# Placing half of batch 6 on TensorE, three copies moved to VectorE, and throw-away matmuls before the first placing

## The reference

```
xh = x.reshape(B, T, 16, 8); xc = xh - mean over tokens
corr = softmax(xc @ xc^T per head); x = layernorm(x + corr @ xh)

scores = sigmoid(x @ gate^T)                 # 64 experts, 8 groups of 8
4 groups are kept (by their two best), 8 experts in them are chosen
w = scores of the 8, normalized, * 2.5
each expert takes its first 128 tokens (CAP): xe[e, pos] = x[token]
ye = (silu(xe @ w1^T) * (xe @ w3^T)) @ w2^T  # F = 64
out = sum over a token's experts of w * ye   # + shared expert (F = 128)
x = layernorm(x + out)
```

## Time and profile before

| | us |
|---|---|
| median of 3 runs | 552.3 (550.35 to 553.13) |
| the profiled execution | 553.05 |
| its span | 550.8 |
| busy: PE, DVE, ACT, POOL | 415.4, 378.3, 365.9, 351.1 |

### The profile page before, as it was taken

One profiled execution on the slowest core, in us unless ns is written; L12 is line 12 of the kernel. 1 busy time (PEld: TensorE's weight loads), 2 busy tenths in 40 slices (PEclk: granted clock), 3 DMA queues, 4 the chain that ended last, 5 costly groups with the idle time before them and its releaser, 6 DMA issues.

```text
span 550.8 us, 9934 instructions
## 1 busy us (share of the span) xinstructions
PE 415.4 (75%) x3461; PEld 185.7 (34%) x3476; DVE 378.3 (69%) x1390; ACT 365.9 (66%) x486; POOL 351.1 (64%) x374
## 2 busy tenths in 40 slices
PE   3799998999898898898899889645699988740000
PEld 2323333333333333333333322123566666530000
DVE  7632769769769768768868638579877887730095
ACT  2699998998998898898998999610223322210056
POOL 3500000677777777777777777777768778888454
PEclk9699999999999999999999999965999999975555
DMA  3499990111000000000100100102366656334796
GB/s 95 139 220 222 349 388 20 52 40 46 24 6 21 14 3 19 12 3 2 27 3 2 26 3 1 24 2 63 78 121 101 112 92 96 36 36 38 150 291 194
DMA packets 71771, 43.69 MB, mean 79 GB/s; under 512 B 11859, under 2 KB 70964, under 8 KB 71329
## 3 DMA queue, kind: packets, MB, share of 16 engines
q1 hardware_dynamic: 51744, 36.18, 24.0%
q0 software_dynamic: 19968, 6.75, 10.5%
HBM read 21.27 MB, written 41.24 MB: 113 GB/s over the span
## 4 chain that ended last, share of the span: by engine, by line
DVE 29%; PE 23%; POOL 16%; ACT 14%; issue 9%; DMA 7%; ACTq 0%; DVEq 0%; POOLq 0%; SPq 0%
POOL records L571 10%; ACT large L1005 9%; PE PV L743 7%; PE S L727 5%; POOL sums L588 5%; DVE large L1587 4%; DMA sums<-centred,target 4%; PE M L645 3%; DVE LR L1261 2%; DVE centred L1644 2%; DMA records<-rec,index 2%; ACT OT L992 1%; PE M L674 1%; DVE last_stats L1672 1%; PE M L668 1%
## 5 line engine op out<-in xcount | busy, mean ns | idle before, releaser
L571 POOL DMA_INDIRECT records<-rec,index x224 | 225.4, 1006 | 141.0 <-DVE index L1404 70.4
L1005 ACT ACTIVATE large<-S,shift 128x1024 f32<-128x1024 f32 x256 | 273.4, 1123 | 23.3 <-PE S L727 21.1
L743 PE MATMUL PV<-large,V 128*9 128x512 f32 x1024 | 135.2, 600 | 0.0
L588 POOL DMA_INDIRECT sums<-centred,target x64 | 99.3, 1552 | 24.9 <-issue 12.2
L727 PE MATMUL S<-LR 64*128 64x512 bf16 x512 | 100.7, 392 | 13.4 <-ACT large L1005 9.0
L727 PEld LDWEIGHTS S<-LR 64*128 64x128 bf16 x512 | 24.6, 93 | 155.1 <-ACT large L1005 98.5
L863 PE MATMUL S<-large 128*128 128x512 bf16 (+1 forms) x189 | 42.6, 375 | 10.0 <-DVE large L1587 6.7
L1261 DVE COPY LR<-M 128x1024 bf16<-128x1024 bf16 x49 | 33.4, 681 | 16.9 <-PE M L645 16.9
L1587 DVE TENSOR_SCALAR large<-slot_c,large 128x128 bf16<-128x128 bf16 x256 | 43.7, 283 | 0.0
L1057 ACT COPY AK<-S 128x512 f32<-128x512 f32 (+1 forms) x17 | 9.5, 560 | 33.6 <-PE S L871 33.6
L863 PEld LDWEIGHTS S<-large 128*128 128x128 bf16 x204 | 19.1, 100 | 29.6 <-issue 9.8
(11 more groups left out here) (207 smaller groups left out, 672.1 us busy)
## 6 DMA issues: line engine op xcount, KB each, us to landing
records<-blank SPq DMA_DIRECT2D x1, 6176.0 KB, 32.2
large<-sums SPq DMA_DIRECT2D x24, 256.0 KB, 5.4
X<-records SPq DMA_DIRECT2D x15, 386.0 KB, 4.4
sums<-blank SPq DMA_DIRECT2D x2, 2112.0 KB
large<-L_ffn_w_dram SPq DMA_DIRECT2D x2, 2048.0 KB, 11.0
records<-rec,index POOLq DMA_INDIRECT x224, 2.1
X<-L_attn_x_dram SPq DMA_DIRECT2D x8, 256.0 KB, 2.9
w2s<-L_ffn_w_dram SPq DMA_DIRECT2D x1, 2048.0 KB, 17.5
```

Source lines behind the costliest of these rows:

```text
L571: pool.indirect_dma_start(records, bass.IndirectOffsetOnAxis(ap=index[:, i * TOP + k:i * TOP + k + 1], axis=0), rec[:, i, :], None, bounds ...
L588: pool.indirect_dma_start(sums[n % SUMS], bass.IndirectOffsetOnAxis(ap=target[:, u, i:i + 1], axis=0), ye[:, u, i, :], None, bounds_check= ...
L743: mm = pe.matmul(PV[g % 2][32 * i:32 * i + VCOLS, :], V[:, b % 2, 2 * c + k, QUAD * g + i, :], E[:, u % 2, i, k, :], start=c == 0 and k == ...
L1005: nc.scalar.activation(E[:, u % 2, 2 * (i // 2):2 * (i // 2) + 2, i % 2, :], S[:, 2 * (n % 2):2 * (n % 2) + 2, :], ACT.Exp, bias=shift[:, ...
```

## The change

Constants: `LATE = 2` tiles of batch 6 (its last two) are placed by PE, so `PLACED = 6` tiles are placed in all. `HOTS = 4` one-hot buffers, `WARM = (20, 26, 10)`, `FIRST_WV = 3`. `TILES_6` are the two tiles of batch 6 and `TILES_7` the four of batch 7 in the operands `x_parts`, `wv`, `slot_of` and `one_hot`, which move to other memory (`x_parts` and `wv` to `Z`, after its stores).

POOL's scatter of batch 6, and what a slot load waits for:

```diff
+                tiles = TILES - LATE if p == BATCHES - 2 else TILES
                 for k in range(TOP):
-                    for i in range(TILES):
-                        n = k * TILES + i
+                    for i in range(tiles):
+                        n = k * tiles + i
...
-            sent = TILES * min(expert + 1, TOP)
+            sent = (TILES - LATE) * min(expert + 1, TOP)
```

PE, after the last attention:

```diff
+            def keep_busy(times):
+                for _ in range(times):
+                    pe.matmul(S[:, 0, :], ident_b[:, :], LR[:, 0, 0, :], start=True, stop=True)
+            pe.wait_ge(exp_done, CHUNKS * BATCHES)
+            keep_busy(WARM[0])
             for name in END_JOBS[:-1]:
                 run_job("epilogue", BATCHES, name)
+            keep_busy(WARM[1])
...
             last_positions()
             run_job("epilogue", BATCHES, END_JOBS[-1])
+            keep_busy(WARM[2])
             def place_x(s, u):
                 n = experts_of(s)
...
-                wait_next(pe, hot, s + 1)
-                if s == 0:
-                    pe.wait_ge(x_split, 4)
-                for k in range(PARTS):
-                    for i in range(TILES):
+                wait_next(pe, hot_late, s + 1)
+                for i in range(PLACED):
+                    if i >= LATE:
+                        wait_next(pe, hot, s * TILES + i - LATE + 1)
+                    if s == 0 and i == 0:
+                        pe.wait_ge(late, LATE_STEPS)
+                    if s == 0 and i == LATE:
+                        pe.wait_ge(x_split, 4)
+                    for k in range(PARTS):
                         pe.matmul(S[:, u % 2, 0:n * CAP], x_parts[:, k, i, :], ...
...
 (find_rows)
+                if s == FIRST_WV + 1:
+                    pe.wait_ge(wv_far, 6)
                 for e in range(experts_of(s)):
-                    for i in range(TILES):
+                    for i in range(PLACED):
```

ACT: `build_v`, `copy_x1T` and `take_turned(6)` leave its list in the attention (the epilogue's `copy_x1T` stays). It makes the one-hots of the two tiles of batch 6, as relu(1 - |c - slot|); `slot_of` holds minus the slot for them:

```diff
+            def late_hot(s, u):
+                n = experts_of(s)
+                if s == 0:
+                    act.wait_ge(unit_weighed, UNITS * BATCHES)
+                    act.wait_ge(late, LATE_SLOTS)
+                if s >= HOTS:
+                    wait(act, found_done, s - HOTS + 1)
+                for i in range(LATE):
+                    for e in range(n):
+                        k = STEP_FIRST[s] + e
+                        ins = nc.scalar.activation(one_hot[:, u % HOTS, i, e, :], slot_c[:, :], ACT.Abs,
+                                                   bias=slot_of[:, i, k:k + 1])
+                ins.then_inc(late_far, 1)
+                wait(act, late_far, s + 1)
+                both = one_hot[:, u % HOTS, 0:LATE, 0:n, :]
+                nc.scalar.activation(both, both, ACT.Relu, bias=1.0, scale=-1.0).then_inc(hot_late, 1)
             copy_quad(BATCHES - 1, QUADS - 1)
             norm_start(BATCHES - 1)
+            late_hot(0, 0)
             copy_x1T("epilogue", BATCHES)
             exp_logits("epilogue", BATCHES, BATCHES - 1)
             exp_gate("epilogue", BATCHES, BATCHES - 1)
+            late_hot(1, 1)
             gate_sigmoid(BATCHES - 1)
+            late_hot(2, 2)
...
             for s in range(STEPS):
                 sigmoid_step(s, s)
                 if s + 1 < STEPS:
                     copy_x(s + 1, s + 1)
                     exp_step(s + 1, s + 1)
+                if s + 1 == FIRST_WV - 1:
+                    act.wait_ge(wv_far, 2)
+                    nc.scalar.copy(part_of(FAR, TILES_7, 0), wv32[:, :, :, FAR]).then_inc(wv_far, 1)
+                if s + 1 == FIRST_WV:
+                    act.wait_ge(wv_far, 4)
+                    nc.scalar.copy(part_of(FAR, TILES_7, 1), wv_rest[:, :, :, FAR]).then_inc(wv_far, 1)
+                if s + 3 < STEPS:
+                    late_hot(s + 3, s + 3)
```

```diff
             last_slot(p, t)
             one_hot_step(0, 0)
+            last_record(p, t)          # now for the experts 0 to 11 alone (NEAR)
             post_shared_out("epilogue", BATCHES, p)
-            last_record(p, t)
-            one_hot_step(1, 1)
-            take_weights(0, 0)
             for s in range(STEPS):
                 add_one(s, s)
+                if s == 0:
+                    one_hot_step(1, 1)
+                    take_weights(0, 0)
+                if s == 1:
+                    first_rows(...)    # weights and numbers of experts 12 to 63 (FAR), 2 instructions
+                if s == FIRST_WV - 1:
+                    far_rest()         # 1 instruction, after ACT's first copy
+                if s == FIRST_WV:
+                    far_low()          # 1 instruction, after ACT's second copy
                 silu_step(s, s)
+                if s < EARLY_STEPS:
+                    weigh_step(s, s)
                 if s + 2 < STEPS:
                     one_hot_step(s + 2, s + 2)
-                weigh_step(s, s)
+                if s >= EARLY_STEPS:
+                    weigh_step(s, s)
```

More of the change, by code:

```diff
@@ L40 @@
 STEPS = len(STEP_FIRST) - 1
+LATE = 2
+PLACED = LATE + TILES
+HOTS = 4
+WARM = (20, 26, 10)
+FIRST_WV = 3
 EARLY_STEPS = 2
@@ L308, in post_norm_block @@
         x_split = sem("x_split")
+        late = sem("late")
+        hot_late = sem("hot_late")
+        late_far = sem("late_far")
+        wv_far = sem("wv_far")
         pos_done = sem("pos_done")
@@ L1013, in batch @@
                             copy_quad(b - 1, QUADS - 1)
[L1014 to L1021, removed]
                     if phase != "first":
@@ L1279, in post_x1, with copy_x1T @@
                                                       ALU.subtract, ALU.mult))
+            def copy_x1T(phase, b):
+                bank, n = job(phase, b, "xt")
+                wait_next(dve, written[bank], n + 1)
+                v.tensor_copy(x1T[:, :], M[bank][:, :]).then_inc(read[bank], 1)
             def post_shared(phase, b, p, t):
@@ L1463, in batch @@
                     post_totals(phase, b, p)
+                if phase == "last":
+                    late_tiles(p, t)
                 if with_prep:
                     take_turned(phase, b, 5)
+                    build_v(b + 1)
                     prep_shift(phase, b, q, w.step, w.after)
@@ L1470, in batch @@
                 if with_prep:
+                    take_turned(phase, b, 6)
                     take_turned(phase, b, 7)
@@ L1546, in last_slot @@
                 dve.wait_ge(pos_read, 1)
-                t.step("slot", v.scalar_tensor_tensor(slot_of[:, :, :], ie(mask), -float(CAP), ie(pos), ALU.mult, ALU.add))
+                t.step("slot", v.scalar_tensor_tensor(slot_of[:, TILES_7, :], ie(mask), -float(CAP), ie(pos),
+                                                      ALU.mult, ALU.add))
             def last_record(p, t):
@@ L1559, in last_record @@
                 t.after("wrec")
-                t.step("recw", v.tensor_tensor(wv32[:, 0, :].rearrange("p (i e) -> p i e", i=TILES), ie(scores),
-                                               wsum[:, :].unsqueeze(2).to_broadcast([P, TILES, EXPERTS]), ALU.mult))
-                token = record_of(p)[0][:, :, TOK_COL]
-                t.step("row", v.scalar_tensor_tensor(wv32[:, 1, :].rearrange("p (i e) -> p i e", i=TILES), ie(pos),
-                                                     float(ALL_TOKENS),
-                                                     token.unsqueeze(2).to_broadcast([P, TILES, EXPERTS]),
-                                                     ALU.add, ALU.subtract))
@@ new lines, in first_rows @@
+            def first_rows(p, step, experts):
+                ie = lambda a: a[:, :].rearrange("p (i e) -> p i e", i=TILES)
+                n = experts.stop - experts.start
+                step("recw", v.tensor_tensor(wv32[:, 0, :, experts], ie(scores)[:, :, experts],
+                                             wsum[:, :].unsqueeze(2).to_broadcast([P, TILES, n]), ALU.mult))
+                token = record_of(p)[0][:, :, TOK_COL].unsqueeze(2).to_broadcast([P, TILES, n])
+                step("row", v.scalar_tensor_tensor(wv32[:, 1, :, experts], ie(pos)[:, :, experts], float(ALL_TOKENS),
+                                                   token, ALU.add, ALU.subtract))
@@ L1581, in one_hot_step @@
                     wait(dve, post, post_at(BATCHES - 1, "slot"))
-                if s >= 4:
-                    wait(dve, found_done, s - 3)
-                for i in range(TILES):
+                if s >= HOTS:
+                    wait(dve, found_done, s - HOTS + 1)
+                for i in range(LATE, PLACED):
                     for e in range(n):
                         own = slot_of[:, i, STEP_FIRST[s] + e:STEP_FIRST[s] + e + 1]
-                        ins = v.tensor_scalar(one_hot[:, u % 4, i, e, :], slot_c[:, :], own, None, ALU.is_equal)
-                ins.then_inc(hot, 1)
+                        ins = v.tensor_scalar(one_hot[:, u % HOTS, i, e, :], slot_c[:, :], own, None, ALU.is_equal)
+                    ins.then_inc(hot, 1)
             split_x(p, t)
```

118 lines of the change are left out of this document (86 added, 32 removed).

## The result

| us | before | after |
|---|---|---|
| median of 4 runs each | 552.71 (550.35 to 556.03) | **565.25** (564.02 to 566.01) |
| the profiled execution | 553.05 | 564.02 |
| its span | 550.8 | 562.3 |

After is to before as 1.0227 (95% interval 1.0189 to 1.0265): slower by 12.5 us. The forecast was 562.0, in a range of 551 to 568.

What follows compares the result with a forecast made beforehand. The prediction took POOL's adds (7.41 us a step) to bound the expert stage; the change's 8.16 us cycle and late early steps gave +11.4 us, less 1.7 from the attention, so 562 us, range 551 to 568.

Steps and rivals of the forecast that it cites:

- The stall at full speed: Full steps: late_hot, 3.6 us between exp and Ln on ACT, makes PE stand 0.9 us; cycle 8.16 us, above POOL's 7.41.
- Scatters: POOL: 16 fewer at 1.27 us each free it 20 us earlier, shortening the time by at most 1 us.
- Moved copies: Attention: copies moved from ACT to DVE in each batch bring -1.7 us in all.
- late_tiles: DVE: 12 instructions, 4.8 us, hidden as they stand before waits of 2.17 and 2.85 us.
- Warm-up and first placing: Epilogue: throw-away matmuls give -0.8 us for DVE's routing; placing 0 ends at 384.3, against 384.9 before.
- Steps 1 to 3: Early steps: late_hot's 3.6 us before each sigmoid and two copies of about 0.5 put step 3's add +5.4 us.
- The sum: Whole kernel: last add +11.4 us, less 1.7 from the attention, +9.7; 562.8 for the profiled execution, 562 us forecast.
- hidden: Rival, expert stage: late_hot costs at most 2.7 us, adds POOL bound from the start; 548.6 us, chance 0.14.
- middle case: Rival, expert stage: steady steps hidden, early steps late, POOL bound from step 3 on; 553.7 us, chance 0.21.
- second table load: Rival, ACT: Abs or Relu needing another load adds 36 us, 598; chance 0.05, shared with low clock in the stalls.

Runs made afterwards that it cites:

- e1: The changed kernel with late_hot(s+3) moved right behind sigmoid_step(s) on ScalarE, all work the same: 554.61 us, ratio 1.0048.
- e4: The changed kernel with two more Abs of 128 columns per step from step 3 on, written where nothing reads: 575.69 us, ratio 1.0427.
- e6: The kernel before with only the three copies moved from ScalarE to VectorE: 552.80 us, ratio 0.9993.
- e7: The kernel before with the throw-away matmuls alone (20, 26 and 10): 554.06 us, ratio 1.0007.
- e10: The kernel before with moved copies, throw-away matmuls and weighing ahead of one-hots up to step 3, no batch 6 tile on PE: 558.00 us, ratio 1.0076.
- e11: The changed kernel with late_hot behind the sigmoid, post_shared_out ahead of last_record, weighing first up to step 3, two tiles kept: 553.04 us, ratio 0.9999.
- e5: The changed kernel with all one-hots on DVE, 24 a step, and no Abs or Relu on ACT: 560.14 us, ratio 1.0113.
- e3: The changed kernel with one tile of batch 6 placed by PE instead of two (LATE = 1): 552.76 us, ratio 1.0026.
- e9: The changed kernel with one batch 6 tile, late_hot behind the sigmoid, post_shared_out ahead of last_record, weighing first up to step 3: 549.36 us, ratio 0.9950.
- e12: e9 with the second group of throw-away matmuls 40 long instead of 26 (WARM = 20, 40, 10): 548.95 us, ratio 0.9923.
- e8: The changed kernel with post_shared_out ahead of last_record and no third group of throw-away matmuls (WARM = 20, 26, 0): 565.25 us, ratio 1.0230.

## Why the prediction was right

*The stall at full speed (the forecast's core).* Right. The cycle was worked out as 8.16 and is 8.00: `late_hot` takes 3.42 us for 3.6 (spacing 0.292 for 0.30, and the Relu, 1.06 long, overlaps the Ln), PE stands 0.69 for 0.9. e1 and e4 show it from both sides.

*Scatters.* Right for this change as far as seen: the last ends at 369.8 (forecast near 373). That by themselves they can give only the 1 us to DVE's line is argued from the rows; no run takes them away alone. What the forecast didn't say, and e6, e7 and e10 show, is that they are what lets any other gain through: with all 224 of them the first add stays at POOL's last scatter.

*Moved copies.* Neither sign nor size is shown. The last index comes at 346.17 for 349.35, 3.2 us earlier, but 1.9 of that are there at the attention's first weighing, ahead of any moved copy (last section). 1.3 is left for 1.7 forecast. But over all profiles of this case the last index comes at 348.0 on the mean of the 12 kernels with the copies moved (346.17 to 350.04) and at 348.3 in the two without (349.35 and 347.25): a gain isn't shown. Counted from the first weighing it is 323.8 us on the mean of the 12 (323.1 to 324.9) and 324.2 in the two: 0.4 us, less than the spread, so the 1.7 wasn't borne out.

*late_tiles.* Right. Its 12 instructions run from 346.45 to 351.04 on DVE, and DVE still waits 0.62 us right behind them, at 352.14.

*Warm-up and first placing.* The step that failed most. The forecast let the placing end at 384.3, or 382.6 with the copies' 1.7 taken off. It ends at 383.86, though the attention was 1.5 us quicker still: from the last index it is 2.8 us late. The main term missed is the wait for DVE's L1425, which the change itself puts behind `last_record`; the earlier trace rows show the same wait before, 2.38 us for L1367, with that instruction still ahead of it. The forecast let the placing start when the ten throw-away matmuls end, 31.1 us after the last index. It starts after 33.6, and in e11, where L1425 stands ahead again, after 31.1. The ten themselves are the smaller term. Their length changes between executions with the same list: 4.2 to 4.4 us here and in e1, e5, e7 and e10, 2.88 to 3.00 in e3, e9 and e11. In e4, where PE stood only 1.78 us before the masks, they take 2.32 us, and yet the placing starts after the same 33.6 us, PE having waited 3.78 us for DVE; it then takes 5.75 us (granted clock 0.73, then 0.64), so this first add came 1.7 us later than the changed kernel's with the ten at 4.40. e12 has the ten at 2.32 and the order of e11, and again it is L1425 that ends last. Whether the program needs this wait ahead of the first placing, which doesn't write `M`, wasn't tried.

*Steps 1 to 3.* The mechanism is right (ACT's 3.5 us ahead of each sigmoid, PE standing, the clock at 1.2 GHz after), and one term too small: the two copies of `wv` with 416 columns were taken as 0.5 us each. ACT's timeline:

```profile
400.29 1.56 ACT L1122 CAST Z<-Z 128x416 bf16<-128x416 f32 x1
401.48 2.49 ACT L1072 ACTIVATE large<-slot_c,AK 128x128 bf16<-128x128 bf16 x8
```

1.19 us from start to start, 0.7 more than forecast, twice. The rest is the clock: behind its stop of 1.96 us at 415.34 PE's up takes 1.98 us for 1.09 (granted clock 0.50 from 416.8 to 418.6), where the forecast had the full clock. From the first add to step 3's it is 26.74 us for 25.5; to step 4's 35.66 for 33.7.

*The sum.* Against the forecast: attention -1.5, last index to first add +3.2, early steps +2.0, ten cycles -1.5 (0.15 each), the last eleven adds 0 (1.853 each, as forecast): +2.2 us for the last add, 527.90 for 525.7. What follows the last add is 34.4 us for 34.8 before. So the profiled execution came out 1.3 us over its forecast (564.02 for 562.8) partly because errors cancelled: a cycle too long by 2% and an attention 1.5 us shorter than forecast, which is luck of this execution, against a start and early steps too short by 5 us. The median, 565.25, is 3.3 us over the forecast of 562.0. Two readings are off and change nothing: the overlap of the ACTIVATEs in the earlier trace rows is (4 x 0.478 - 1.65) / 3 = 0.087 and not 0.094, and the 1.54 / 9 for a one-hot stands in no row, whose 2.68 / 16 is the same 0.17.

*The rivals.* Of "hidden" the limit was right: in e1, where `late_hot` is off PE's path, it costs nothing in the steady steps. What the forecast didn't see is that its middle case, no change, is what one moved line of the program makes true. A second table load didn't come: the profile has one ACT_TABLE_LOAD, 1.28 us, as before. The Trainium skill, "ScalarE: Activation LUTs", section "Table sets: the hidden batching unit", says that abs and relu are in every set; the trace agrees. Its section "Rules for kernel authors", by which relu and the like belong on VectorE, goes by the price of an instruction. That price is borne out here, the advice isn't: DVE makes a one-hot in 3.99 / 24 = 0.17 us against 0.29 for the Abs alone, yet the kernel with the work on DVE (e5) has a ratio of 1.0113 and the one with it on ACT behind the sigmoid (e1) 1.0048; from the last index to the last add they take 177.1 and 170.8 us.

## What to carry to other kernels

- Where an in-order engine gets new work, ask first what stands behind it in that engine's list and who waits for that. The same nine instructions a step cost some 10 us in one place and nothing that the rows of the full steps show in another, and idle time of that engine (ACT works 5.08 of the 8.00 us) says nothing about it.
- Throw-away matmuls help only on the path that ends last (e7: nothing). Behind a pause they run at half speed themselves (4.40 us for 2.32), and they still paid where PE would have stood anyway: the clock was back for the matmuls that count (e8 against e11: 2.1 us).
- When a start is moved forward, list every other thing that the moved step waits for; here it was one instruction on DVE, moved back by the same change, and it took up to 2.5 us of the gain.

## What the runs showed of the hardware

**A start that differs from execution to execution.** The first score matmuls of the two profiled executions are the same code:

```profile
19.19 0.61 PE L727 MATMUL S<-LR 64*128 64x512 bf16 x2 [2.56 <-issue]
```

```profile
18.47 0.39 PE L745 MATMUL S<-LR 64*128 64x512 bf16 x2 [2.56 <-issue]
```

The first row is before, at 1.2 GHz, the second after, at 2.4 GHz. At the first weighing the difference is 1.9 us (24.95 against 23.04), and it isn't made good later. Of the 14 profiled executions six show the first and eight the second, and e7, with the attention of the kernel before, is among the eight: it isn't the change. In the profiled executions of ten kernels with the same attention code the last index lies between 346.2 and 350.0, a good part of the spread of one kernel's runs (550.35 to 556.03). Times of single executions can't tell 1% here; distances from a landmark of the same execution, such as last index to first add, can.

**A strided copy.** 128x416 from f32 to bf16 on ACT takes 1.56 us where the source and the target are in pieces; 128x1024 from bf16 to bf16 in one piece, in the kernel before, takes 1.02. Two CASTs of DVE in that kernel, both 128x512 from f32 to bf16, point the same way: 1.02 us where the target is every sixth element of `wv` (L1569), 0.43 where it is whole rows (L1532). ACT has no such pair here, so for its 1.56 us the pieces are a likely cause and not a shown one.

**A placing that begins at the low clock** and regains the high one on the way takes 6.67 us (e8, granted clock 0.50, then 0.68) or 5.35 (step 3's in the changed kernel, 0.74 on the mean) for 4.06.
